# Keys and values of two attention layers projected inside an earlier stage, and two stages reordered

## The reference

```python
x = x + jnp.tanh(g_xattn[0]) * _L0_xattn_ref(_layernorm(x, axis=-1), ctx_1024, ctx_1024)     # retention
x = x + jnp.tanh(g_ffn[0]) * _L0_ffn_ref(_layernorm(x, axis=-1), ...)                         # switch attention
x = x + jnp.tanh(g_xattn[1]) * _L1_xattn_ref(ctx_1024, _layernorm(x, axis=-1))                # distances, warp, align
x = x + jnp.tanh(g_ffn[1]) * _L1_ffn_ref(_layernorm(x, axis=-1), weight_q, weight_scale, bias)
x = x + jnp.tanh(g_xattn[2]) * _L2_xattn_ref(_layernorm(x, axis=-1), ctx_1024, mask, Wq, bq, Wk, bk, ...)
x = x + jnp.tanh(g_ffn[2]) * _L2_ffn_ref(_layernorm(x, axis=-1), ...)                         # low rank
x = x + jnp.tanh(g_xattn[3]) * _L3_xattn_ref(_layernorm(x, axis=-1), ctx_1024, ctx_1024, Wq, bq, Wk, bk, ...)
x = x + jnp.tanh(g_ffn[3]) * _L3_ffn_ref(_layernorm(x, axis=-1), ...)                         # mixture of experts

# _L1_xattn_ref, per batch, on the distances D between context and x:
r = d_ij + jnp.minimum(jnp.minimum(up, left), diag)          # cost table, row by row
# then back from the last corner to the origin: argmin of diag, up, left at each step
expanded = jnp.zeros((T_large, d)).at[j_idx].add(contrib)    # context rows summed along the path
x_scale = jnp.maximum(amax, EPS) / 127.0
x_q = jnp.clip(jnp.round(x2d / x_scale), -128, 127).astype(jnp.int8)
out = (x_q @ weight_q.T).astype(jnp.float32) * x_scale * weight_scale[None, :] + bias
# _L2_xattn_ref (_L3_xattn_ref has no rel and no mask)
q, k, v = x @ Wq + bq, y @ Wk + bk, y @ Wv + bv              # 16 heads of 16
attn = (einsum(q + r_w_bias, k) + shift(einsum(q + r_r_bias, pe))) * (1.0 / math.sqrt(HEAD_DIM))
p = jax.nn.softmax(attn * mask - 10000000000.0 * (1.0 - mask))
out = einsum(p, v) @ Wo + bo
```

## Time and profile before

| | us |
|---|---|
| median of 3 runs | 1896.55 (1895.06 to 1896.75) |
| the profiled execution | 1886.68, span 1884.7 |
| PE busy | 1382.4 (73%) |
| DVE busy | 1237.1 (66%) |
| ACT busy | 560.5 (30%) |
| POOL busy | 343.5 (18%) |

### The profile page before, as it was taken

One profiled execution on the slowest core, in us unless ns is written; L12 is line 12 of the kernel. 1 busy time (PEld: TensorE's weight loads), 2 busy tenths in 40 slices (PEclk: granted clock), 3 DMA queues, 4 the chain that ended last, 5 costly groups with the idle time before them and its releaser, 6 DMA issues. The chain is left out here.

```text
span 1884.7 us, 32009 instructions
## 1 busy us (share of the span) xinstructions
PE 1382.4 (73%) x9677; PEld 1160.8 (62%) x9677; DVE 1237.1 (66%) x3141; ACT 560.5 (30%) x1628; POOL 343.5 (18%) x484
## 2 busy tenths in 40 slices
PE   3668999999999966100002359999789899979998
PEld 2337888888888855100001137777678699868887
DVE  5875776677776757696595748888645466535554
ACT  2331212112221113000000017777423576623232
POOL 4750000000000001000001114444323111122221
PEclk9668999999999985555555569999889999989999
DMA  5541212112121124202307227777422111100000
GB/s 186 172 144 30 57 29 53 31 29 56 29 51 33 29 74 125 46 0 37 75 0 215 78 80 180 192 193 187 105 62 67 49 51 50 35 22 17 22 17 17
DMA packets 176323, 137.73 MB, mean 73 GB/s; under 512 B 16818, under 2 KB 170243, under 8 KB 173892
## 3 DMA queue, kind: packets, MB, share of 16 engines
q1 hardware_dynamic: 158864, 119.75, 24.5%
q10 hardware_dynamic: 17396, 17.23, 3.2%
HBM read 100.87 MB, written 36.06 MB: 73 GB/s over the span
## 5 line engine op out<-in xcount | busy, mean ns | idle before, releaser
L720 DVE TENSOR_TENSOR moa_oe<-moa_mask,moa_ogT 128x1024 fp32r<-128x1024 bf16 x128 | 155.4, 1225 | 35.7 <-PE moa_k_ps L93 32.6
L1142 PE MATMUL warp_t_ps<-ident,warp_entry 128*128 128x128 f32 x1 | 0.5, 477 | 220.8 <-DVE warpb_hit L1125 220.8
L91 PE MATMUL moa_k_ps<-moa_w_out_hi,moa_oe 128*128 128x256 f32 x512 | 150.2, 293 | 13.6 <-DVE moa_oe L720 13.6
L92 PE MATMUL moa_k_ps<-moa_w_out_lo,moa_oe 128*128 128x256 f32 x512 | 143.8, 281 | 0.0
L93 PE MATMUL moa_k_ps<-moa_w_out_hi,moa_oe 128*128 128x256 f32 x512 | 143.4, 280 | 0.0
L1142 PEld LDWEIGHTS warp_t_ps<-ident,warp_entry 128*128 128x128 f32 x1 | 0.2, 183 | 221.1 <-DVE warpb_hit L1125 221.1
L1851 PE MATMUL L_b_ps<-L_v,L_pT 128*128 128x128 f32 x1024 | 127.3, 282 | 1.4 <-DVE L_xo L1538 0.8
L1851 PEld LDWEIGHTS L_b_ps<-L_v,L_pT 128*128 128x128 f32 x1024 | 121.9, 197 | 6.8 <-issue 6.8
L91 PEld LDWEIGHTS moa_k_ps<-moa_w_out_hi,moa_oe 128*128 128x128 f32 x512 | 96.9, 189 | 22.7 <-issue 16.9
L1681 ACT ACTIVATE L_xnT<-L_b_ps 128x256 f32<-128x256 f32 x16 | 5.8, 365 | 352.0 <-PE L_b_ps L1773 352.0
L687 DVE COPY_PREDICATED moa_v_sel<-moa_onehot,moa_y_ps 128x512 f32<-128x512 int32 x112 | 82.2, 734 | 40.0 <-DVE moa_v_sel L687 29.8
(11 more groups left out here) (334 smaller groups left out, 3780.4 us busy)
## 6 DMA issues: line engine op xcount, KB each, us to landing
bounce<-L_rel SPq DMA_DIRECT2D x64, 258.0 KB, 4.1
moa_mask<-chosen SPq DMA_DIRECT2D x32, 512.0 KB, 5.9
L_shifted<-bounce SPq DMA_DIRECT2D x64, 256.0 KB, 4.3
ret_staged_values<-in_w_value_dram ACTq DMA_DIRECT2D x8, 512.0 KB, 3.7
ret_staged_outputs<-in_w_out_dram ACTq DMA_DIRECT2D x8, 512.0 KB, 4.0
ret_cT<-in_ctxT_pairs_dram SPq DMA_DIRECT2D x16, 256.0 KB, 2.8
L_x<-x_after SPq DMA_DIRECT2D x32, 128.0 KB, 2.2
L_cT<-in_ctxT_pairs_dram SPq DMA_DIRECT2D x32, 128.0 KB, 2.7
```

The lines of the kernel that those rows point to most:

```text
L91: pe.matmul(out, x_hi, w_hi, start=first, stop=False)
L92: pe.matmul(out, x_hi, w_lo, start=False, stop=False)
L720: dve.tensor_tensor(oe[e % 2][:, :, :, :].rearrange("p a m s -> p a (m s)"), mask[:, e, :, :].rearrange("p m s -> p (m s)").unsqueeze(1).t ...
```

## The change

1. The weights of layer 3's attention, eight transfers on ACT's queue, are loaded in the distance stage behind layer 2's, no longer in the int8 stage.
2. `ContextProjection` runs inside the warp's two blocks, on PE and ACT: batches 0 to 7 in the first, 8 to 15 in the second. Per batch PE makes keys and values of both layers, the value bias coming from a product with one row of ones; ACT copies them with the key bias, for layer 3 in the masked form `kz`, and stores them to scratches in DRAM on its own queue. The second block ends when all stores have landed.
3. The warp works in blocks of rows: the distances in three loads, the costs in four store-and-load rounds within the first block, the steps in three stores and three loads. The path stays in SBUF, where the int8 stage reads it. The warp has 41 semaphores instead of 13.
4. The int8 stage: DVE's operations of three batches are interleaved (`in_deep_phases`); the copy of `qT` is ACT's, behind its weight loads; the gate is folded into scale and bias once; the bias and the final sum are POOL's.
5. Layers 2 and 3 project queries alone. SP loads keys and values from the scratches. In layer 2, DVE and ACT make the two halves of `kz` from the loaded keys, one operation each; in layer 3 the loaded keys are used as they are.

```diff
-                later_weights.load(act)
+                for w_later in later_weights:
+                    w_later.load(act)
...
+    def load(self, act, n, u):
+        act.dma_start(self.cT[u][:, :, :], self.k.ins["ctxT_pairs"][n, 0].rearrange("(t p) s -> p t s", p=128)).then_inc(self.cT_loaded[u], 16)
+    def project(self, pe, n, u):
+        pe.wait_ge(self.cT_loaded[u], loads(n, u))
+        for layer in range(2):
+            weights, out = self.weights[layer], self.kv_ps[layer][u]
...
+            for m in range(DT):
+                for t in range(DT):
+                    pe.matmul(out[:, m * S:m * S + S], weights.wk[:, t, 128 * m:128 * m + 128], self.cT[u][:, t, :],
+                              start=(t == 0), stop=(t == DT - 1))
+            for t in range(DT):
+                pe.matmul(out[:, D:2 * D], self.cT[u][:, t, :], weights.wv[:, t, :], start=(t == 0), stop=False)
+            pe.matmul(out[:, D:2 * D], self.first_row[:, :], weights.bv[:, :], start=False, stop=True).then_inc(self.kv_done[layer], 1)
...
+    def store(self, act, n, u):
...
+        act.wait_ge(self.kv_done[0], after(n + 1))
...
+        for t in range(DT):
+            act.activation(self.kT[u][:, t, :], self.kv_ps[0][u][:, t * S:t * S + S], ACT.Identity,
+                           bias=self.weights[0].bk[:, t:t + 1])
+        self.copy_values(act, 0, u).then_inc(self.kv_out[0], 1)
+        act.wait_ge(self.kv_done[1], after(n + 1))
+        if n + 2 < B:
+            self.load(act, n + 2, u)
...
+        for t in range(DT):
+            for par in range(2):
+                act.activation(self.kz[u][:, t, par, :], self.kv_ps[1][u][:, t * S:t * S + S], ACT.Identity,
+                               bias=self.key_bias[:, par, t:t + 1], scale=self.k.pair_mask[:, par:par + 1])
+        self.copy_values(act, 1, u).then_inc(self.kv_out[1], 1)
...
+        act.dma_start(self.projected[0].keys[n], self.kT[u][:, :, :]).then_inc(self.kT_stored[u], 16)
+        act.dma_start(self.projected[0].values[n], self.v[0][u][:, :, :]).then_inc(self.values_stored[0][u], 16)
...
+        act.dma_start(self.projected[1].keys[n], self.kz[u][:, :, :, :]).then_inc(self.kz_stored[u], 16)
+        act.dma_start(self.projected[1].values[n], self.v[1][u][:, :, :]).then_inc(self.values_stored[1][u], 16)
...
+        LOADS = ((0, 8), (8, 40), (40, S))
+        COSTS = ((0, 64), (64, 104), (104, 120), (120, S))
+        STEPS = ((112, S), (64, 112), (0, 64))
...
-                    sp.dma_start(dd[:, :, :].rearrange("b i j -> b (i j)"), dist.rearrange("b i j -> b (i j)")).then_inc(dist_in, 16)
-                    sp.dma_start(iota_j[:, :], k.ins["c_iota"]).then_inc(dist_in, 16)
+                    for (r0, r1), landed in zip(LOADS, dist_in):
+                        sp.dma_start(dd[:, r0:r1, :], dist[:, r0:r1, :]).then_inc(landed, 16)
+                    sp.dma_start(iota_j[:, :], k.ins["c_iota"]).then_inc(iota_in, 16)
...
+                    for (r0, r1), written in zip(COSTS, costs_out):
+                        sp.wait_ge(row_ready, after(r1))
+                        sp.dma_start(costs[:, r0 + 1:r1 + 1, :], rr[:, r0:r1, :]).then_inc(written, 16)
+                        sp.wait_ge(written, after(16))
+                        sp.dma_start(cost[r0:r1, :, :], costs[:, r0 + 1:r1 + 1, :].rearrange("b i j -> i b j")).then_inc(tables_in, 16)
+                        sp.dma_start(above[r0:r1, :, :], costs[:, r0:r1, :].rearrange("b i j -> i b j")).then_inc(tables_in, 16)
+                    sp.wait_ge(tables_in, after(32 * len(COSTS)))
...
+                @block.scalar
+                def _(act):
+                    for n in range(2):
+                        projection.load(act, n, n)
+                    for n in range(B // 2):
+                        projection.store(act, n, n % 2)
+                @block.tensor
+                def _(pe):
+                    for n in range(B // 2):
+                        projection.project(pe, n, n % 2)
...
-                    sp.dma_start(steps.rearrange("b i j -> i b j"), nxt[:, :].rearrange("p (b j) -> p b j", j=S)).then_inc(steps_out, 16)
-                    sp.wait_ge(steps_out, after(16))
-                    sp.dma_start(chase[:, :, :].rearrange("b i j -> b (i j)"), steps.rearrange("b i j -> b (i j)")).then_inc(steps_in, 16)
...
+                    for (r0, r1), written in zip(STEPS, steps_out):
+                        sp.dma_start(steps[:, r0:r1, :].rearrange("b i j -> i b j"),
+                                     nxt[r0:r1, :].rearrange("p (b j) -> p b j", j=S)).then_inc(written, 16)
+                    for (r0, r1), written, landed in zip(STEPS, steps_out, steps_in):
+                        sp.wait_ge(written, after(16))
+                        sp.dma_start(chase[:, r0:r1, :], steps[:, r0:r1, :]).then_inc(landed, 16)
...
+                def step(b, u, ahead=True, front=True, middle=True, tail=True):
+                    if ahead:
+                        ln.inverse_root(pool, b + 2)
+                    if middle:
+                        pool.wait_ge(xab_ready, after(b + 1))
+                        pool.wait_ge(scaled_ready, after(b + 1))
...
+                        pool.tensor_tensor(xo[u][:, :], scaled[:, u, :], xab[:, u, :], ALU.add).then_inc(xo_ready, 1)
+                    if ahead:
+                        pool.wait_ge(xa_ready, after(b + 3))
...
+                        pool.tensor_tensor(xab[:, u, :], xa[:, u, :], gated_bias[:, :], ALU.add).then_inc(xab_ready, 1)
...
+                        act.wait_ge(qT_ps, after(b + 2))
+                        act.wait_ge(acc_done, after(b + 1))
+                        act.activation(qT[:, :, :], t_ps[:, 0:D].rearrange("p (t s) -> p t s", s=S), ACT.Identity,
+                                       bias=minus_round[:, :]).then_inc(qT_ready, 1)
...
+                        dve.tensor_scalar(scale[:, nu:nu + 1], amax[:, :], QEPS, 1.0 / QMAX, ALU.max, ALU.mult).then_inc(step_done, 1)
+                    if middle:
+                        dve.wait_ge(acc_done, after(b + 1))
...
+                        dve.scalar_tensor_tensor(scaled[:, u, :], a_ps[:, 0:D], scale[:, u:u + 1], scaled_weight[:, :],
+                                                 ALU.mult, ALU.mult).then_inc(scaled_ready, 1)
+                    if front:
...
+                dve.wait_ge(weights_in, after(48))
+                dve.tensor_scalar(scaled_weight[:, :], w_scale[:, :], k.gates[:, 5:6], None, ALU.mult).then_inc(setup, 1)
+                dve.tensor_scalar(gated_bias[:, :], bias[:, :], k.gates[:, 5:6], None, ALU.mult).then_inc(setup, 1)
...
+                def load_keys(n, v_):
+                    target = kT[v_][:, :, :] if relative else kz[v_][:, :, :, :]
+                    sp.dma_start(target, projected.keys[n]).then_inc(keys_loaded[v_], 16)
+                def load_values(n, v_):
+                    sp.dma_start(v[:, v_, :, 0:HALF * VD], projected.values[n]).then_inc(values_loaded[v_], 16)
...
-                    if ahead and (not isinstance(b, int) or -2 < b < B - 3):
-                        sp.wait_ge(v_done, after(b + 2))
-                        load_context(b + 3, nu)
+                    if ahead and (not isinstance(b, int) or b >= 0):
+                        if relative:
+                            sp.wait_ge(k_ready, after(b + 1))
+                            sp.wait_ge(k_ready_act, after(b + 1))
+                        else:
+                            sp.wait_ge(s_done, after(b * 4 + 4))
+                        load_keys(b + 2, u)
+                    if front and (not isinstance(b, int) or b >= 1):
+                        sp.wait_ge(pv_done, after(b))
+                        load_values(b + 1, nu)
...
-                def keys(n):
-                    dve.wait_ge(k_ready_act, after(n + 1))
+                def keys(n, v_):
+                    dve.wait_ge(keys_loaded[v_], loads(n, v_))
                     dve.wait_ge(s_done, after(n * 4))
...
-                def values(n, v_):
-                    dve.wait_ge(v_done, after(n + 1))
-                    dve.wait_ge(pv_done, after(n - 1))
-                    dve.tensor_tensor(heads_of(v[:, v_, :, :])[:, :, :, 0:HD], by_half(v_at), by_half(bv[:, :]),
-                                      ALU.add).then_inc(v_ready, 1)
+                    dve.tensor_scalar(kz[0][:, :, 0, :], kT[v_][:, :, :], k.pair_mask[:, 0:1], None, ALU.mult).then_inc(k_ready, 1)
...
-                def copy_odd_keys(n):
-                    act.wait_ge(qk_done, after(n + 1))
+                def copy_odd_keys(n, v_):
+                    act.wait_ge(keys_loaded[v_], loads(n, v_))
                     act.wait_ge(s_done, after(n * 4))
-                    for t in range(DT):
...
+                    act.activation(kz[0][:, :, 1, :], kT[v_][:, :, :], ACT.Identity, bias=zero[:, :],
+                                   scale=k.pair_mask[:, 1:2]).then_inc(k_ready_act, 1)
...
-                def queries_and_keys(n, v_):
```

(4 more changed lines are left out.)

358 lines of the change are left out of this document (203 added, 155 removed).

## The result

The changed kernel took 1838.25 us, the median of 4 runs (1833.98 to 1839.09), against 1896.34 for the kernel before: 58 us less, a ratio of 0.969 (0.9673 to 0.9707). The forecast was 1824, its range 1797 to 1856. The profiled execution took 1838.59, span 1836.4.

A forecast was written before the change was run, and what follows sets the result against it. Limits differ by stage: DVE alone in the warp, PE in layer 3, a chain through the mask in layer 2. Distances +5, warp −35, int8 −23, layer 2 0, layer 3 −20 sum to −73: 1896.55 − 73 = 1824, range 1797 to 1856.

The forecast's parts named there:

- R2: Rival, covers leak: layer 2's key wait costs 1 us a step, +14, the warp +10; 1848 us, chance 0.15.
- Warp, −35: Warp stage: (a) to (d) together sum to −34.9 us, from −24 to −42.
- (a): Warp's start: DVE's first row needs 64 KB instead of 1 MB of distances and comes earlier, −7.5 us.
- (b): Warp, last row to tables: only the last 8 rows' store and loads remain, 5.8 instead of 21.3 us, −15.5.
- (d): Warp's end: the path stays in SBUF, so its store goes, −3.9 us.
- (c): Warp, before the first lookup: the wait for stored and reloaded steps falls from 16.55 to 8.5 us, −8.
- R4: Rival: warp rows and lookups slow by 0.3 us each beside PE, ACT and transfers; about 1896 us, chance 0.03.
- int8, −23: int8 stage: DVE loses 1.96 us a step, −29 over fifteen steps, and a later start adds +6.
- Layer 2, 0: Layer 2: PE's 2.1 us less a step not counted, another chain closes the step; ends +10 and −8.
- R1: Rival: PE bounds layer 2, so 2.1 × 14 = −29 us more; 1795 us, chance 0.10.
- R3: Rival: layer 2's clock falls to 1.2 GHz with less PE work, +121 us, net +48; 1945 us, chance 0.04.
- Layer 3, −20: Layer 3: PE's own step loses 1.2 us, keys 1.06 and values 0.15, 19 over 16 steps, 1 at the start.

The follow-up runs named there:

- a1: Changed kernel, ACT issuing the weights of layers 2 and 3 at the warp's start, key bias set between rows 24 and 25: 1832.38 us.
- w1: Changed kernel with all sixteen batches projected in the warp's first block and none in the second: 1832.57 us, one run.
- e3: Kernel before, with layer 2's mask of batch b+2 loaded ahead of the bounce's writes: 1878.21 us against 1891.03, ratio 0.9936.
- e2: Changed kernel with layer 2's keys loaded one step earlier and its mask loaded ahead of the bounce's writes: 1819.24 us, ratio 0.9602.
- f1: Changed kernel plus two unread 128x256 PE products a step right behind layer 2's queries: 1832.38 us against 1827.01 on the same chip.
- b2: Changed kernel with the edits of e2, w1 and a1 together, plus two unread 128x256 PE products ahead of layer 2's relative products: ratio 0.9543.
- g0: Kernel before, unchanged, profiled again on the chip that also ran g1: 1892.10 us.
- g1: Changed kernel, unchanged, profiled again on the chip of g0: 1827.01 us against 1892.59, ratio 0.9655.
- w2: Changed kernel with SP storing and loading the first block of steps before issuing the other two blocks' stores: 1834.14 us, one run.

## Why the prediction was right, and where it was off

The direction and the range were right, the likeliest case was 14 us too fast by the recorded medians, 7 on one chip. But the prediction called itself wrong if layer 2's period moved by more than 1 us or its clock fell, and in the first profile both came: 14.3 to 15.7 us, and 1.00 to 0.95. On one chip the period moved by 0.6 and the clock was 0.98 over 14 steps. What came lies between the likeliest case and R2, with its key wait of 1 us a step (the steps grew by 0.6 to 1.4) and a part of its leak in the warp (4 us of 10). The total is inside the likeliest case's own end of 1842 although layer 2's +16.5 in the first profiles is beyond the +10 stated for it, so the total alone doesn't speak for the working.

- **Distances, +5:** 5.8 measured, by the mechanism named (a1).
- **Warp, −35:** −31.0. (a) the first row: −7.6 for −7.5. (b) the tables: the 21.3 us became 6.6, −14.7 for −15.5; the pieces named there (1.7, 1.7, two issues of 0.4 and some 2) add up to 6.2 and not to the 5.8 used. (d) −4.1 for −3.9. (c) is the step that was mis-sized: the wait became 12.1, not 8.5, −4.4 for −8. Its bound to the slow side, "ACT's transfers beside them", was the case: w1 takes them away and gets 8.8. The transfers show it: 128 KB of steps took 8.3 us to load.

```profile
steps<-warpb_nxt SPq DMA_DIRECT2D x1, 128.0 KB, 3.8
...
warpb_chase<-steps SPq DMA_DIRECT2D x1, 128.0 KB, 8.3
```

   The Trainium skill's rule of the prediction (DMA: Bandwidth & Descriptors, Queues, rings and completion order) pointed this way; the 12.1 lies between the 8.5 without sharing and the 14 of transfers doubled throughout. The cover held: behind the first projections a batch took 4.4 us, at a granted clock of 0.97 to 1.00 from 787 to 817, and R4's slower rows didn't come (97.2 us, 97.0 before; a lookup 340 ns in both).
- **int8, −23:** −24.2, with the step at 3.88 us, but not by the working. DVE's operations without slowing would add up to about 3.4. Its normalisation and clipping run beside POOL's new additions and take twice as long:

```profile
L229 DVE TENSOR_SCALAR int_ln_xn<-int_xa,int_ln_mv,int_ln_rstd 128x256 f32<-128x256 f32 x10 | 9.5, 949 | 0.0
L1416 DVE TENSOR_SCALAR int_clipped<-int_shifted 128x256 f32<-128x256 f32 x11 | 7.9, 720 | 0.4
```

```profile
993.61 0.40 DVE L229 TENSOR_SCALAR int_ln_xn<-int_xa,int_ln_mv,int_ln_rstd 128x256 f32<-128x256 f32 x1
...
1009.42 0.95 DVE L229 TENSOR_SCALAR int_ln_xn<-int_xa,int_ln_mv,int_ln_rstd 128x256 f32<-128x256 f32 x1
1009.49 0.73 POOL L1361 TENSOR_TENSOR int_xab<-int_xa,int_gated_bias 128x256 f32<-128x256 f32 x1
```

   The first of these is the one normalisation of the stage that overlaps no addition of POOL's: 0.40 us; the 15 others took 0.80 to 0.95. Clipping took 0.29 where it overlapped none. That is some 0.95 us a step. The number is right by luck: two errors of about a microsecond met, waits between dependent operations that went, which I had not counted, and this.
- **Layer 2, 0:** +4.3 on one chip, +16.5 between the first profiles. The step that failed is "Against the step of 14.06, the key chain adds up to some 14.4": no sum stands behind the 14.4, and even its 0.3 was then costed at 0. The wait was seen (keys landing at 1219.1 for a copy at 1216.46), but ACT, SP and the bounce form a circle, as the rows of one step show, and a late copy delays the next step's issue too: the steps were 15.2 to 15.7 us. That the mask, and not PE, closed the step of before is shown by e3, and R1, by which layer 2 would be 29 us shorter, is refuted by the result and by e2.
- **R3** came in a small form: the clock didn't fall for the stage, but dipped in some steps, at up to 1.6 us for a weighing. What brings a dip is open as a cause, since f1 and b2 had next to none to remove. But dips go with PE's pauses: over the last 14 steps of layer 2 in each of the 14 profiles, the granted clock fell below 0.93 in 20 of the 29 steps whose longest pause of PE was 2.0 us or more, and in 2 of the 124 in which none reached 1.5 us.
- **Layer 3, −20:** −18.1 (−16.6 between the first profiles). The step fell from 10.52 to 9.46, by 1.06 and not by 1.2. From one group of products to the next the keys had taken 0.89 of PE's time and not the 1.06 of their busy span, the values 0.87; 0.50 of that came back just ahead of the transposition of x, where PE now pauses for the normalisation that the value product covered before, and about 0.2 in slightly longer gaps between other groups. On the one chip 15 steps give −15.3, the start and the end of the stage −2.9. The pause:

```profile
1510.61 0.44 PE L1941 MATMUL L_a_ps<-ident,L_ln_xn 128*128 128x128 f32 x2 [0.35 <-DVE L_ln_xn L229]
```

The rest of the gap to 1824 is the difference between 58 us less in the first runs and 66 on the chip of g0 and g1. The profile of after is 12.4 us longer than g1, and 9.7 of these lie in layer 2 (281.1 against 271.4). Why the same layer 2 takes 271.4 to 281.3 us in five profiles isn't shown; dips alone don't order them (two of 14 steps for 271.4 and also for 278.2 in w2). The fast end of the likeliest case's range is a slip: its bounds, added as independent, give 1809 and not 1806.

## What to carry to other kernels

Work taken from a busy engine is worth time only if that engine closes the step: follow the circle of waits once around, here mask, weighing, bounce, mask, before counting a busy share of 96% as a bound, and then look for the next circle, which here, with the key load in it, was the longer one by 0.6 us a step. A load that replaces a computed operand should be issued early enough to land before the instruction that wants it, here a step earlier, above all where that instruction stands in front of others on an in-order engine. Transfers that are hidden behind compute on their own queue can still lengthen the short waits of another queue, so put them beside a stretch in which nobody waits for a transfer.

## What the runs showed of the hardware that was not expected

Two of DVE's operations with one tensor in SBUF took about twice as long beside POOL's additions: the normalisation took 949 ns in the int8 stage of after, and 407 for the same shape in the int8 stage of before, when POOL made no additions; the one in after that overlapped none took 401. The operation that makes `shifted`, a third of the kind, kept its 0.35 us in the 12 steps in which an addition began 0.13 us or more behind its start. The Trainium skill (SBUF — State Buffer, section SBUF: two separate sides) says that a DVE operation in a two-port mode and one of GpSimd exclude each other on a shared port pair; these rows agree with it, though no run shows in which mode they ran, and moving work to POOL should have been charged with it.

The same kernel differed by up to 11 us between chips (medians of before 1885.46 to 1896.34), and by up to 8 us between executions on one chip (1891.48 to 1899.66). In its three profiles the warp is equal within 0.4 us and layer 2 lies between 264.6 and 267.9.
